# A two-layer decoder on one core: the first layer's film, modulation and spectrum go tile by tile into the selection loop, and its inverse, norms and feed forward are done per batch half

## The chip, the cores and the metric

The kernel runs on one core of a Trainium2 chip. The metric is the device time of one execution in microseconds, as the median of several runs. Engines: PE (matrix products), DVE (vector), ACT (scalar), POOL (GpSimd), SP (issues DMAs). Every engine has its own instruction stream, executes it in order, and waits on semaphores.

## The reference, cut to what matters

Two decoder layers over x (2 x 512 x 128) with a context of 2 x 154 x 96. The change lies in the second block of the first layer, and at its edges:

```python
scores = einsum('bthd,bghd->bhtg', Q, K) / sqrt(32)        # 4 heads, 154 keys
topv, topi = top_k(scores, 32); probs = softmax(topv)      # the selection
attn_mean = attn.mean(axis=1)
c_t = einsum('btg,bgd->btd', attn_mean, x_vision @ Wv) * text_mask
x = layernorm(x_text, g_norm_in, b_norm_in)
scale_in, shift_in = split(c_t @ W_film_in + b_film_in)    # film
x = x * (1 + mod_gate * scale_in) + mod_gate * shift_in    # modulation
y = irfft(rfft(x, 2L) * rfft(K, 2L))[:, :L] + x * D_skip   # K: taps from 64 states
y = y * (1 + mod_gate * scale_out) + mod_gate * shift_out
xt = x_text + y
h = gelu(layernorm(xt, g_ffn, b_ffn) @ W1 + b1) @ W2 + b2
return layernorm(xt + h, g_norm_out, b_norm_out)
```

After it come the outer norm, a mixture of experts over the same rows, and the second layer.

## The kernel before, in words

The 1024 rows are 8 tiles of 128 rows, tiles 0 to 3 being batch half 0 and tiles 4 to 7 half 1. PSUM is 8 banks of 512 columns. There is no scheduler: each engine's order is written out by hand in one function per stage, and the semaphores carry the dependences.

**Selection (b_pe_attention, b_dve_attention, b_act_attention).** Per tile, PE makes the scores (score, L658 and L660), ACT copies them (scores_in, L831), DVE finds each head's maximum (peak), ACT takes the exponentials (L841, L842), and DVE finds the 32 largest of each of 4 heads with rounds of max and match_replace (select), and makes probabilities (selected, shares; the last instruction of a tile is the reciprocal L808). ACT then makes four diagonal matrices (diagonals, L846 and L853), PE gathers the transposed attention (gather, L683 and L686), ACT copies it (attn_in, L902 and L903), PE multiplies by the film weights (film_tile, L708 and L709) and ACT copies the 512 film columns (film_in, L859). PE puts film_tile one tile behind, and a dummy product (stay_warm, L217) ahead of each gather.

**Taps.** Beside the selection ACT makes exponential and sine tables (low rates L497, high rates L504, waves L510 to L519), POOL multiplies them (L440 to L467), PE turns them into 512 taps (taps_of_lags, L669, at tile TAPS_AT = 5), ACT copies them in 16 small pieces (b_act_taps, L529), PE takes their spectrum (taps_spectrum, L721, with an outer product for D_skip, L723), and ACT weighs it (b_act_spectrum, L475).

**Modulation and spectrum.** POOL makes the affine norm u_n (L922 to L924) and modulates tiles 0 to 3 at once (L930, L931); DVE modulates tiles 4 to 7 (L987, L988) after the norm of the context (L982). PE takes the spectrum (L695) after all films.

**After it (b_pe_ssm, b_dve_ssm, b_act_ssm).** DVE multiplies the spectra in 4 groups of both halves (L996 to L1001), PE inverts (L939, L944, moving operand 256 columns), DVE applies the film (L1010 to L1013) and norms (stats L176, aggregate L179, variance L181, POOL's power L197, scaling L187), PE transposes (L209), ACT copies (L972), PE widens by W1 (L956), ACT takes gelu (L975), PE narrows by W2 (L963, the bias as an outer product L961), DVE adds and takes two norms per half (L1023 onward). PE meanwhile merges the experts' weights (c_pe, L1066 and L1072) and then transposes the rows (L209 again), which needs DVE's last norm: from there on the change touches nothing but a bank number.

Of the kernel before, what the change touches and what calls it, by code (L numbers as in the profile page):

```python
# [73 lines left out]
LINES = [("ffn_b2", 128), ("m_ob", 128), ("l_bo", 128), ("b_film", 512)]  # L74
# [23 lines left out]
def _build(nc, dram, ctx):  # L98
# [40 lines left out]
    ones_low = keep(64).bitcast(BF16)[0:1, :]  # L139
# [52 lines left out]

    def pool_rstd(pool, n=NT):
# [30 lines left out]
    def a_sp(sp):  # L224
# [9 lines left out]
        sp.dma_start(SB[0:1, r0 + 1024:r0 + 1024 + 896], dram["lines"]).then_inc(sem("small_in"), 16)  # L234
# [234 lines left out]
    def b_act_spectrum(act):  # L469

        act.wait_ge(sem("s_taps_dft"), 1)
        w = lambda j: ssm["bin_weight"][:, j:j + 1]
        for out, i in ((taps_re, 0), (taps_im2, 1), (taps_re2, 0)):
            for j in range(4):
                ins = act.activation(out[:, 128 * j:128 * j + 128], bank(i)[:, 128 * j:128 * j + 128], ACT.Copy, scale=w(j))  # L475
        ins.then_inc(sem("s_spectrum"), 1)
        act.wait_ge(sem("s_spectrum"), 1)
        act.activation(taps_re2[0:1, 0:128], bank(1)[0:1, 0:128], ACT.Copy, scale=w(0)[0:1, :])
        act.activation(taps_im2[0:1, 0:128], ones[0:1, :], ACT.Copy, scale=0.0).then_inc(sem("s_spectrum"), 1)

# [41 lines left out]
    def b_act_taps(act):  # L522
# [4 lines left out]
        for q in range(4):  # L527
# [74 lines left out]
    def b_pool_pre(pool, follow):  # L602
# [12 lines left out]
        follow(pool.tensor_copy(ones_low, ones[0:1, :]))  # L615
        follow(pool.tensor_scalar(skip_line, skip_line, 0.5, None, ALU.mult))
# [21 lines left out]
    hT = inner  # L638
    gelu = film


    FILMS = [[], [0], [1], [2], [3], [4], [5], [7]]
    TAPS_AT = 5

    def b_pe_attention(pe):
# [27 lines left out]
        def gather(t):  # L673

            if t >= 2:
                pe.wait_ge(sem("x_attn_in"), 2 * (t - 1))
# [3 lines left out]
            o = bank(4 + t % 2)  # L680
# [10 lines left out]
        def spectrum(part, j, b):  # L691

            mat = dft[("dft_cos", "dft_sin")[part]]
            for c in range(4):
                ins = pe.matmul(bank(4 * part + j)[:, 128 * b:128 * b + 128],  # L695
                                mat[:, 512 * c + 128 * j:512 * c + 128 * j + 128], uv[:, b, c], start=(c == 0), stop=(c == 3))
            return ins

        def film_tile(t):
# [5 lines left out]
            if t >= 2:  # L705
                pe.wait_ge(sem("x_film_in"), t - 1)
            b = t // (NT // B)
            pe.matmul(bank(6 + t % 2), attn0[:, 128 * t:128 * t + 128], vf0[:, 512 * b:512 * b + 512], start=True, stop=False)  # L708
            pe.matmul(bank(6 + t % 2), attn1[0:33, 128 * t:128 * t + 128], vf1[0:33, 512 * b:512 * b + 512], start=False,  # L709
                      stop=True).then_inc(sem("x_film"), 1)  # L710

        def taps_spectrum():

            pe.wait_ge(sem("x_scores_in"), NT)
            pe.wait_ge(sem("s_taps_copied"), 16)
            pe.wait_ge(sem("dft_in"), 16)
            for part, mat in ((0, dft["dft_cos"]), (1, dft["dft_sin"])):
                for j in range(4):
                    o = bank(part)[:, 128 * j:128 * j + 128]
                    for c in range(4):  # L720
                        ins = pe.matmul(o, mat[:, 512 * c + 128 * j:512 * c + 128 * j + 128],  # L721
                                        taps[:, 128 * c:128 * c + 128], start=(c == 0), stop=False)
                    ins = pe.matmul(o, mat[0:1, 128 * j:128 * j + 128], skip_line, start=False, stop=True)  # L723
# [1397 lines left out]
```

## Time and profile before

| what | value |
|---|---|
| median of 3 runs | 797.09 us (796.39 to 802.22) |
| profiled execution | 796.2 us |
| its span, first to last instruction | 794.1 us |
| mean granted clock of PE | 0.951 |
| PE busy | 713.8 us, 90% |
| DVE busy | 456.4 us, 57% |
| ACT busy | 279.5 us, 35% |
| POOL busy | 226.1 us, 28% |
| stretch that the change touches | about 36 to 220 us |

The span is the time between the first and the last instruction; what lies around it is 2.1 us. A view of a stretch starts its clock at the span's start. A float matrix product of 128 columns shows as two records, so that 8 records are 4 products. A start in one row and the start in the next give the time for which an engine is held; the duration in a row is a little longer where instructions overlap.

### The profile page before, as it was taken

What the parts mean: (1) busy time and instruction counts of PE and PEld (TensorE: products, weight loads), DVE (VectorE), ACT (ScalarE), POOL (GpSimd) and SP (SyncE); (2) the same over time, 40 slices, a digit from 0 to 9 for tenths busy, and PEclk for the clock granted to TensorE, in tenths of its full rate; (3) what the DMA queues carried; (4) which work ended last, traced back from release to release, by engine and by line L of the source; (5) the groups of instructions that cost most, each with busy time, mean ns of one, the idle gap of its engine ahead of it and who ended that gap; (6) DMA issues with size and microseconds to landing.
All of it is one profiled execution on the core that took longest, in us unless ns stands there. A gap on an engine that the chain in (4) does not pass through costs nothing.

```text
span 794.1 us, 8963 instructions
## 1 busy us (share of the span) xinstructions
PE 713.8 (90%) x3296; PEld 355.4 (45%) x3296; DVE 456.4 (57%) x1190; ACT 279.5 (35%) x527; POOL 226.1 (28%) x135
## 2 busy tenths in 40 slices
PE   8675879898989989999999999999977989999996
PEld 5232447774845433322222222227432354656555
DVE  7898890423626684576676767743664635333333
ACT  7998663003021004544444444430213204121220
POOL 4728710001201020435454554641635010000001
PEclk9867889999998999999999999999998989999999
DMA  8100050011000000000000000000500000000000
GB/s 314 32 0 1 1 213 1 1 60 47 1 1 0 1 0 0 1 1 0 1 1 0 1 1 0 1 1 1 225 1 0 1 1 1 1 0 1 1 0 28
DMA packets 3493, 18.67 MB, mean 24 GB/s; under 512 B 887, under 2 KB 2040, under 8 KB 2938
## 3 DMA queue, kind: packets, MB, share of 16 engines
q1 hardware_dynamic: 3450, 18.11, 5.9%
q8 instruction: 26, 0.43, 0.2%
q14 instruction: 17, 0.14, 0.1%
HBM read 17.58 MB, written 0.52 MB: 23 GB/s over the span
## 4 chain that ended last, share of the span: by engine, by line
PE 68%; DVE 14%; ACT 10%; issue 4%; POOL 3%; DMA 1%; POOLq 0%; DVEq 0%; SPq 0%; ACTq 0%
PE PS L1840 10%; PE PS L1323 7%; PE PS L1854 6%; DVE SB L1477 5%; PE PS L1307 4%; PE PS L1278 4%; PE PS L1291 3%; DVE SB L1226 2%; PE PS L695 2%; PE PS L217 2%; PE PS L1339 2%; PE PS L1361 2%; PE PS L1406 2%; PE PS L1638 2%; PE PS L1649 1%
## 5 line engine op out<-in xcount | busy, mean ns | idle before, releaser
L197 POOL TENSOR_TENSOR SB<-SB 128x4 f32<-128x4 f32 (+1 forms) x24 | 23.9, 997 | 371.6 <-DVE SB L181 371.5
L1460 POOL TENSOR_TENSOR SB<-SB 128x1024 f32<-128x1024 f32 x32 | 75.2, 2351 | 127.7 <-ACT SB L1430 127.6
L1477 DVE TENSOR_REDUCE SB<-PS 128x2 f32<-128x1024 f32 x64 | 78.5, 1226 | 52.7 <-PE PS L1291 52.6
L1430 ACT ACTIVATE SB<-PS 128x1024 f32<-128x1024 f32 x64 | 65.6, 1024 | 105.2 <-PE PS L1310 105.1
L217 PE MATMUL PS<-SB 128*128 128x512 f32 (+1 forms) x190 | 86.7, 602 | 1.5 <-DVE SB L294 1.1
L1840 PE MATMUL PS<-SB 128*128 128x512 f32 x176 | 82.5, 607 | 0.0
L1307 PE MATMUL PS<-SB 64*128 64x512 f32 x256 | 68.9, 616 | 0.0
L1323 PE MATMUL PS<-SB 128*64 128x512 f32 x256 | 67.8, 610 | 1.2 <-DVE SB L1514 1.2
L1510 DVE RECIPROCAL SB<-PS 128x512 f32<-128x512 f32 x16 | 53.7, 3358 | 17.6 <-PE PS L1339 17.6
L1920 DVE TENSOR_TENSOR SB<-SB,PS 128x512 f32<-128x512 f32 (+1 forms) x48 | 32.9, 688 | 52.7 <-PE PS L1840 48.9
L1878 ACT ACTIVATE SB<-PS 128x512 f32<-128x512 f32 (+1 forms) x48 | 28.5, 596 | 87.3 <-PE PS L1840 85.8
L1854 PEld LDWEIGHTS PS<-SB 128*128 128x128 f32 (+1 forms) x384 | 49.4, 190 | 18.5 <-issue 10.0
L1854 PE MATMUL PS<-SB 128*128 128x128 f32 (+1 forms) x384 | 54.5, 285 | 1.4 <-DVE SB L1920 1.4
L217 PEld LDWEIGHTS PS<-SB 128*128 128x128 f32 x190 | 36.2, 213 | 35.8 <-issue 32.5
L1840 PEld LDWEIGHTS PS<-SB 128*128 128x128 f32 x176 | 31.3, 189 | 33.4 <-issue 29.2
L1464 POOL TENSOR_TENSOR SB<-SB 128x1024 f32<-128x1024 f32 x16 | 37.6, 2348 | 1.3
L1278 PE MATMUL PS<-SB 128*128 128x512 f32 x64 | 35.8, 641 | 0.3 <-ACT SB L1413 0.3
L1307 PEld LDWEIGHTS PS<-SB 64*128 64x128 f32 x256 | 22.0, 187 | 27.2 <-issue 24.3
L1323 PEld LDWEIGHTS PS<-SB 128*64 128x64 f32 x256 | 14.4, 135 | 42.8 <-issue 33.0
L683 PE MATMUL PS<-SB 128*128 128x128 f32 x64 | 12.7, 362 | 18.6 <-ACT SB L853 18.6
L1291 PE MATMUL PS<-SB 64*128 64x512 bf16 x128 | 24.8, 384 | 4.6 <-DVE SB L1477 4.6
L1928 DVE SCALAR_TENSOR_TENSOR SB<-PS,SB 128x128 f32<-128x128 f32 x32 | 11.2, 351 | 30.3 <-PE PS L1854 30.3
(356 smaller groups left out, 1144.2 us busy)
## 6 DMA issues: line engine op xcount, KB each, us to landing
SB<-exp SPq DMA_DIRECT2D x1, 4352.0 KB, 13.2
SB<-moe SPq DMA_DIRECT2D x1, 4096.0 KB, 12.9
SB<-dft SPq DMA_DIRECT2D x1, 2304.0 KB, 11.6
SB<-att SPq DMA_DIRECT2D x1, 2048.0 KB, 8.1
SB<-mix SPq DMA_DIRECT2D x1, 768.5 KB, 4.7
SB<-mix SPq DMA_DIRECT2D x1, 640.0 KB, 5.8
SB<-ssm SPq DMA_DIRECT2D x1, 602.0 KB, 6.8
SB<-lat SPq DMA_DIRECT2D x1, 585.0 KB
```

The source lines that it names most:

```text
L217: pe.matmul(bank(b)[:, 0:moving.shape[1]], ones, moving, start=True, stop=True)
L1278: pe.matmul(bank(7), w[:, 128 * pair:128 * pair + 128], xsT[:, 512 * b:512 * b + 512], start=True, stop=True)\
L1291: ins = pe.matmul(bank(4 + h), qb_ring[i % 3][head(h), 128 * qt:128 * qt + 128], kb_ring[i % 3][head(h), :], start=True, stop=True)
L1307: pe.matmul(bank(2 * (n % 2) + h), k_ring[i % 3][head(h), 128 * u:128 * u + 128], q_ring[i % 3][head(h), :], start=True, stop=False)
L1323: ins = pe.matmul(bank(6)[head(h), :], v, expd[i % 2][:, 1024 * kt + 512 * h:1024 * kt + 512 * h + 512], start=(kt == 0), stop=(kt == 3))
L1430: act.activation(expd[i % 2][:, 1024 * u:1024 * u + 1024], bank(2 * (u % 2), 2), ACT.Exp).then_inc(sem("d_exp"), 1)
L1460: pool.tensor_tensor(half_sums[half], e[:, 0:1024], e[:, 1024:], ALU.add).then_inc(sem("d_half_sum"), 1)
L1464: pool.tensor_tensor(key_sum, half_sums[0], half_sums[1], ALU.add).then_inc(sem("d_key_sum"), 1)
L1477: dve.tensor_reduce(shift[i % 2][:, qt:qt + DK + 1:DK], two_heads(bank(4, 2)), AX_X, ALU.max, negate=True)\
L1510: dve.reciprocal(unit, bank(7)).then_inc(sem("d_unit"), 1)
L1840: pe.matmul(bank(2 * (i % 3) + side), exp_w["e_w13"][:, c:c + 128], xsT[:, 512 * n:512 * n + 512], start=True, stop=True).then_inc(sem(("t ...
L1854: ins = pe.matmul(bank(6 + j % 2)[:, 0:128], hidden[e % 2][0:m, T * k + 128 * t:T * k + 128 * t + 128], w2, start=(k == 0), stop=(k == FCH ...
```

## The change

The film of a tile follows its gather at once, all films in bank 6, all gathers in bank 4, and the dummy products in the selection are gone. POOL makes u_n ahead of its tap products and modulates tiles 0 to 6 one by one among them; DVE modulates tile 7 straight from PSUM. PE takes the spectrum tile by tile, accumulating over a half's tiles in two banks per half (5 and 7, 2 and 3), which a product with a row of zeros opens. The taps are made at tile 4 instead of 5, and ACT copies them in two groups of 8. D_skip is added to tap 0 by POOL. The taps' spectrum follows film 5 and DVE weighs it instead of ACT. Products, inverse, film, norm, transposes, widening, gelu and narrowing go per half; the inverse's moving operand is 128 columns. The stream x is added to the film's shift by POOL, POOL keeps the sum with the bias b2, and the outer products of D_skip and b2 are gone, for which the biases are now loaded to all 128 partitions. The second batch of low rates on ACT moves from tile 0 to tile 2. The context's norm on DVE comes after tile 7's modulation.

```diff
-        sp.dma_start(SB[0:1, r0 + 1024:r0 + 1024 + 896], dram["lines"]).then_inc(sem("small_in"), 16)
+        sp.dma_start(SB[:, r0 + 1024:r0 + 1024 + 384], dram["lines"][:, 0:384].to_broadcast([P, 384])).then_inc(sem("small_in"), 16)
...
+        follow(pool.memset(zeros_low, 0.0))
...
+    TAPS_AT = 4
+    SPECTRA = ((5, 7), (2, 3))
...
-            stay_warm(pe, 1, 4 + t % 2)
...
+        def spectrum(t):
+            b, c = divmod(t, 4)
+            if t < NT - 1:
+                pe.wait_ge(sem("s_u"), t + 1)
+            else:
+                pe.wait_ge(sem("s_u_late"), 1)
...
+            if c == 0:
+                for i in SPECTRA[b]:
+                    pe.matmul(bank(i), zeros_low, mask_low[:, 0:512], start=True, stop=False)
+            for part, mat in enumerate((dft["dft_cos"], dft["dft_sin"])):
+                for j in range(4):
+                    ins = pe.matmul(bank(SPECTRA[b][part])[:, 128 * j:128 * j + 128],
+                                    mat[:, 512 * c + 128 * j:512 * c + 128 * j + 128], uv[:, b, c], start=False, stop=(c == 3 and j == 3))
...
             if t == TAPS_AT:
                 taps_of_lags()
+                spectrum(1)
+                spectrum(2)
+            gather(t)
+            if t == 3:
+                spectrum(0)
             if t == NT - 1:
...
+                spectrum(4)
+            film_tile(t)
+            if t == TAPS_AT:
+                spectrum(3)
             if t == TAPS_AT + 1:
                 taps_spectrum()
...
+        for t in (5, 6, 7):
+            spectrum(t)
...
+            if t >= 2:
+                film_in(t - 2)
+            if t > TAPS_AT:
+                attn_in(act, t - 1)
...
             if t == TAPS_AT + 1:
-                b_act_taps(act)
+                b_act_taps(act, 2, 4)
             if t + 1 < NT:
                 exponentials(2 * t + 3)
-            if t >= 1:
+            if 1 <= t <= TAPS_AT:
                 attn_in(act, t - 1)
...
-            if t == 0:
+            if t == 2:
                 b_act_low_rates(act, 16, LOW)
             if t == 3:
                 b_act_high_rates(act)
+            if t == TAPS_AT:
+                b_act_taps(act, 0, 2)
         diagonals(NT - 1)
-        b_act_spectrum(act)
...
+        b_pool_high_factor(pool, follow, 0)
+        b_pool_high_factor(pool, follow, 1)
+        modulate(0)
+        b_pool_high_factor(pool, follow, 2)
+        b_pool_low_factor(pool, 0)
+        modulate(1)
+        b_pool_low_factor(pool, 1)
+        b_pool_high_factor(pool, follow, 3)
+        modulate(2)
+        modulate(3)
+        pool.wait_ge(sem("s_taps_copied"), 16)
+        pool.tensor_tensor(taps[0:1, 0:128], taps[0:1, 0:128], skip_line, ALU.add).then_inc(sem("s_taps_in"), 1)
+        modulate(4)
+        modulate(5)
+        modulate(6)
...
+        for b in range(B):
+            pe.wait_ge(sem("s_product"), b + 2)
+            if b == 1:
+                pe.wait_ge(sem("x_film_in"), NT)
+            y = bank(4 + 2 * b)
...
+        turn(0)
+        stay_warm(pe, 1, 0)
+        widen(0)
+        turn(1)
+        narrow(0)
+        widen(1)
+        narrow(1)
...
+        dve.wait_ge(sem("s_spectra"), 1)
+        products(0)
+
+        last = NT - 1
+        dve.wait_ge(sem("u_affine"), 1)
+        dve.wait_ge(sem("x_film"), NT)
+        follow(dve.tensor_tensor(tiled(u)[:, last], tiled(u_n)[:, last], bank(6)[:, 0:128], ALU.mult))
+        dve.tensor_tensor(tiled(u)[:, last], tiled(u)[:, last], bank(6)[:, 128:256], ALU.add).then_inc(sem("s_u_late"), 1)
...
+        dve.wait_ge(sem("s_spectra"), 2)
         dve.memset(dft["dft_sin"].rearrange("p (c l) -> p c l", c=4)[:, 1:4, 0:1], 0.0).then_inc(sem("s_product"), 1)
-
...
+        products(1)
...
+            follow(dve.tensor_tensor(tiled(inner)[:, tiles], four(bank(4 + 2 * b)), fv[:, tiles, 2], ALU.mult))
+            ins = dve.tensor_tensor(tiled(inner)[:, tiles], tiled(inner)[:, tiles], fv[:, tiles, 3], ALU.add)
+            ins.then_inc(sem("f_inner"), 1)
+            dve.wait_ge(sem("f_inner"), b + 1)
+            norm_half(dve, follow, tiled(inner), tiled(inner_n), b).then_inc(sem(("f_half", "f_normed")[b]), 1)
...
+            dve.wait_ge(sem("f_inner_kept"), k + 1)
             dve.wait_ge(sem("f_out"), k + 1)
...
+            follow(dve.tensor_tensor(xsum[:, c], xsum[:, c], bank(4 + 2 * k), ALU.add))
+            follow(norm_half(dve, follow, tiled(xsum), tiled(xn), k))
+            follow(dve.tensor_tensor(tiled(xn)[:, tiles], tiled(xn)[:, tiles], every(rows["g_out"]), ALU.mult))
+            follow(dve.tensor_tensor(xsum[:, c], xn[:, c], u_n[:, c], ALU.add))
+            norm_half(dve, follow, tiled(xsum), tiled(xs), k).then_inc(sem(("stage_half", "stage_done")[k]), 1)
...
-        sp.wait_ge(sem("s_conv"), 4)
+        sp.wait_ge(sem("s_conv"), 2)
```

norm_half is the norm of one half by the same instructions as before, with its own wait for POOL's power. POOL's list behind the selection (b_pool_ssm) is: x into the shift of half 0, the two powers of the context's norm, x into the shift of half 1, x plus b_out for all rows, then for each half the power and the sum with b2, then four powers.

## Rows read from the trace of the kernel before

**Rows 1.** Windows: us, busy of PE, PEld, DVE, ACT, POOL; clock, DMA, GB/s
```profile
36.00:53.00 17.00, 11.56 (x26) 5.22 (x27) 16.68 (x92) 16.16 (x60) 8.07 (x2) 0.50 0.00 0
...
205.60:220.00 14.40, 14.40 (x130) 12.76 (x130) 11.57 (x46) 1.02 (x1) 3.07 (x3) 1.00 0.01 1
```

**Rows 2.** Chain of work that ended last: start us, us, what
```profile
104.07 0.39 ACT SB L529
...
120.22 1.09 PE PS L721 x8
...
160.05 1.99 PE PS L939 x8
...
174.16 1.30 DVE SB L1010 x2
...
180.97 1.04 POOL SB L197
182.04 1.13 DVE SB L187 x4
...
185.16 7.15 PE PS L956 x16
...
205.60 7.15 PE PS L1066 x64
...
219.88 1.04 PE PS L209 x8
```

**Rows 3.** Timeline of DVE: start us, us, instruction, [idle before, releaser]
```profile
86.47 0.54 DVE L761 MAX8 SB<-SB 128x8 f32<-128x154 f32 x2 [1.95 <-ACT SB L831]
...
115.94 0.17 DVE L808 RECIPROCAL SB<-SB 128x4 f32<-128x4 f32 x1
...
199.70 0.69 DVE L1023 TENSOR_TENSOR SB<-SB,PS 128x512 f32<-128x512 f32 x1 [14.80 <-PE PS L963]
...
201.74 0.17 DVE L181 TENSOR_SCALAR SB<-SB 128x4 f32<-128x4 f32 x1
```

**Rows 4.** Timeline of ACT in the selection
```profile
57.43 1.90 ACT L510 ACTIVATE SB<-SB 128x2048 f32<-128x2048 f32 x1
...
79.26 0.60 ACT L859 ACTIVATE SB<-PS 128x512 f32<-128x512 f32 x1 [2.09 <-PE PS L709]
79.75 3.73 ACT L504 ACTIVATE SB<-SB 128x128 f32<-128x128 f32 x16
83.28 0.27 ACT L846 ACTIVATE SB<-SB 128x4 f32<-128x4 f32 x1
...
84.76 0.41 ACT L841 ACTIVATE SB<-SB 128x154 f32<-128x154 f32 x1
...
85.77 0.66 ACT L831 ACTIVATE SB<-PS 128x616 f32<-128x616 f32 x1
...
104.07 6.64 ACT L529 ACTIVATE SB<-PS 32x128 f32<-32x128 f32 x16 [1.89 <-PE PS L669]
```

**Rows 5.** Timeline of PE in the selection
```profile
85.00 2.05 PE L683 MATMUL PS<-SB 128*128 128x128 f32 x8 [2.83 <-ACT SB L853]
...
92.02 0.79 PE L658 MATMUL PS<-SB 128*128 128x308 f32 x2
...
94.88 1.05 PE L683 MATMUL PS<-SB 128*128 128x128 f32 x8
...
96.85 1.12 PE L708 MATMUL PS<-SB 128*128 128x512 f32 x2
...
98.96 2.14 PE L669 MATMUL PS<-SB 128*32 128x16 f32 x232
```

**Rows 6.** Timeline of POOL in the selection
```profile
62.63 7.44 POOL L453 TENSOR_TENSOR SB<-SB 128x2048 f32<-128x2048 f32 x2 [18.56 <-ACT SB L512]
...
83.72 4.54 POOL L458 TENSOR_TENSOR SB<-SB 128x2048 f32<-128x2048 f32 x1
...
99.81 1.10 POOL L930 TENSOR_TENSOR SB<-SB 128x512 f32<-128x512 f32 x1 [4.82 <-ACT SB L859]
```

More of the change, by code:

```diff
@@ L138, in _build @@
     key_bytes, key_columns = [bytes_in[r:r + 1, 2048:2048 + B * S2] for r in (0, DK)], bytes_in[:, NT:NT + 2 * B]
-    ones_low = keep(64).bitcast(BF16)[0:1, :]
+    ones_low, zeros_low = (keep(64).bitcast(BF16)[0:1, :] for _ in range(2))
     stream = Space(keep.at, keep.at + 4096)
@@ L526, in b_act_taps @@
         to = taps.rearrange("p (c g j) -> p c g j", c=4, j=4)
-        for q in range(4):
+        for q in range(a, z):
             for j in range(4):
@@ L858, in film_in @@
                 act.wait_ge(sem("s_low_products"), 3)
[L859 removed]
+            if t == NT - 1:
+                act.wait_ge(sem("s_u_late"), 1)
+            act.activation(film[:, 512 * t:512 * t + 512], bank(6), ACT.Copy).then_inc(sem("x_film_in"), 1)
         scores_in(0)
@@ L968, in b_act_ssm, with modulate @@
-    def b_act_ssm(act):
-        act.wait_ge(sem("turned"), 2)
-        act.wait_ge(sem("ffn_in"), 16)
-        act.wait_ge(sem("f_inner_kept"), 1)
-        act.activation(hT, bank(4, 2), ACT.Identity, scale=ffn["ffn_g"], bias=ffn["ffn_b"]).then_inc(sem("turned_in"), 1)
-        for k in range(4):
-            act.wait_ge(sem("f_hidden"), k + 1)
-            act.activation(gelu[:, T * k:T * k + T], bank(2 * (k % 2), 2), ACT.Gelu, bias=ffn["ffn_b1"][:, k:k + 1])\
-               .then_inc(sem("f_gelu"), 1)
+        def modulate(t):
+            pool.wait_ge(sem("x_film_in"), t + 1)
+            follow(pool.tensor_tensor(tiled(u)[:, t], tiled(u_n)[:, t], film[:, 512 * t:512 * t + 128], ALU.mult))
+            pool.tensor_tensor(tiled(u)[:, t], tiled(u)[:, t], film[:, 512 * t + 128:512 * t + 256], ALU.add).then_inc(sem("s_u"), 1)
@@ new lines, in b_act_ssm @@
+    def b_act_ssm(act):
+        act.wait_ge(sem("ffn_in"), 16)
+        for h in range(2):
+            c = slice(512 * h, 512 * h + 512)
+            act.wait_ge(sem(("x_half_turned", "turned")[h]), 2)
+            act.activation(hT[:, c], bank(5 + 2 * h), ACT.Identity, scale=ffn["ffn_g"], bias=ffn["ffn_b"])\
+               .then_inc(sem(("x_half_in", "turned_in")[h]), 1)
+            if h == 0:
+                act.wait_ge(sem("f_inner"), 2)
+            for k in range(4):
+                act.wait_ge(sem("f_hidden"), 4 * h + k + 1)
+                act.activation(gelu[:, T * k + 512 * h:T * k + 512 * h + 512], bank(k), ACT.Gelu, bias=ffn["ffn_b1"][:, k:k + 1])\
+                   .then_inc(sem("f_gelu"), 1)
@@ L1025, in b_dve_ssm @@
-        follow(norm(dve, follow, tiled(xsum), tiled(xn), prepare=add))
-        follow(dve.tensor_tensor(tiled(xn), tiled(xn), every(rows["g_out"]), ALU.mult))
-        follow(dve.tensor_tensor(xsum, xn, u_n, ALU.add))
-        norm(dve, follow, tiled(xsum), tiled(xs), first_half="stage_half").then_inc(sem("stage_done"), 1)
+            tiles = slice(4 * b, 4 * b + 4)
+            dve.wait_ge(sem("s_conv"), b + 1)
+            dve.wait_ge(sem("x_film_in"), 4 * b + 4)
+            dve.wait_ge(sem("s_shift"), b + 1)
@@ L1990, in _ @@
         b_pool_attention(pool, follow)
-        pool_rstd(pool, 4)
-        for _ in range(3):
-            pool_rstd(pool)
+        b_pool_ssm(pool)
         for _ in range(3):
```

247 lines of the change are left out of this document (119 added, 128 removed).

## Prediction

> **What bounds the kernel now.** I read the windows first, then the chain of work that ended last between 36 and 220 us, then the timelines of the four engines there. Up to tile 7 DVE's selection is nearly gapless: in the window 36 to 53 it is busy 16.68 of 17 us [rows 1], and its last reciprocal stands at 115.94 [rows 3]. But the chain leaves DVE at tile 5: the taps end on PE at 104.04, ACT begins 16 copies at 104.07 [rows 2], which last 6.64 us [rows 4], and tile 6's gather and the films queue behind them. From 120.22 PE works alone: the taps' spectrum, film 6, gather 7, the spectra. The inverse begins at 160.05, 44 us after the selection ended; it ends at 174.16, when DVE takes the film's product [rows 2]. Then DVE and PE take turns (film and norm, then the widening from 185.16). From 205.60 PE has 14.3 us of merging (two groups like that of 205.60, 7.15 us each) beside DVE's norms, and at 219.88 it transposes the finished rows [rows 2]. That start is the point where both kernels meet again: behind it the program is the same and TensorE sets the pace, so what it moves by, the end moves by.
>
> **Prices.** A product of 128x128 on 128 columns: 7.15 us for 64 records, so 0.2234 us each [rows 2]; where small products stand between, 1.09 us for 8 records, 0.2725 each at L721 [rows 2]. I take 0.2234 for runs of one kind (new inverse, narrowing, taps' spectrum, spectrum), since they are such runs, and keep 0.2725 for the range. With TensorE at full clock a gather is 1.97 us (94.88 to 96.85), a film 2.11 (96.85 to 98.96), a tile's scores 1.9 (from 92.02 to 94.88 stand they and a dummy of 0.96) [rows 5]; at half clock the first half of a gather is 2.05 instead of 1.0 at 85.00 [rows 5]. ACT: film copy 0.49, sixteen rates 3.53, diagonals 1.48, one pair of exponentials 1.0, scores copy 0.6 [rows 4]; attention copy about 0.35, an estimate from the width (film copy 0.49 is wider, twice 0.17 at least); a tap copy 0.415 [rows 4].
>
> **The start.** The bias load becomes a broadcast of 192 KB, and POOL gets one more memset. That delays POOL's list by 0.6 us or so by the volume; POOL, DVE and PE stand at most as late as ACT there, which is busy without a gap until it copies the first half of x. I take 0, at most 0.5.
>
> **Leg 1, to the end of the taps on PE.** ACT: 3.5 us of low rates leave tile 0; so the waves start when DVE's second tile lets them, about 1.4 us before 57.43 (1.9 gained, 0.5 for the film copy that now stands ahead). POOL: u_n (three instructions over 1024 columns, 6.6 us by twice the 1.10 for 512) goes into the 18.56 us of idle ahead of 62.63, which hides it; two modulations enter its products, 0.7 us each (from 1.10 us for 512 columns [rows 6]; 128 columns are between a quarter, 0.28, and 1.10 for each of two instructions, I take 0.35). POOL's products then end at 88.26 - 1.4 + 1.4 = 88.3 [rows 6]: unchanged, no bound. ACT in tile 3's turn: waves end at 67.9, exponentials and copy 1.35, low rates 3.53, diagonals 1.48, 2.1 for exponentials, scores and film, 1.35 again, high rates 3.53, diagonals 3 at 82.8. PE then does gather 3, spectrum 0, film 3, scores 7: 1.97 + 2.3 + 2.11 + 1.9 = 8.3 us warm, 16 us cold; PE stands idle for ACT ahead of gather 3, and the gather after such a wait ran at the lower clock at 85.00, so I add 2: the taps start at 93.1 and take 5.08 us as before (98.96 to 104.04, with the fetch in the middle [rows 2, 5]). They end at 98.2 instead of 104.04. Bounds 96.3 and 104.
>
> ACT waits for exactly that: its first 8 tap copies stand ahead of diagonals 4 and of the scores copy 7. DVE goes on with tile 5 (its exponentials are done) until about 96, then waits for the scores of tile 7 until about 104: some 7 us of DVE idle, against 1.95 and less now [rows 3]. The selection ends near 123 instead of 116. This is the price of the earlier taps, and PE's own queue hides it (next leg).
>
> **Leg 2, ACT to gather 5.** 8 x 0.415 = 3.3, diagonals 1.5, then the longer of gather 4 (2 to 4) and exponentials, scores copy, film copy (2.1), attention copy 0.35, taps 3.3, exponentials 1.0, diagonals 1.5: 13.1 + 0.7 = 13.8. Gather 5 starts at 112.0.
>
> **Leg 3, PE to the last spectrum.** Gather 5 3.0 (half cold), hand-over 0.45, film 5 2.1, taps' spectrum 32 x 0.2234 = 7.15 (12.0 before, 120.22 on, with the D_skip products), gather 6 1.97, hand-over 0.45, film 6 2.1, gather 7 2.0, opening products 0.5, spectrum 4 1.8, film 7 2.1, spectra 5 to 7 5.4: 29.0, end at 141.0. DVE's end of selection at 123 is 6 us ahead of gather 7 (129). Tile 7's modulation (0.5) is hidden by spectra 5 and 6; the taps' weights and half 0's products (2.3 + 4.1 on DVE: three and six instructions over 512 columns at 0.69 or less [rows 3], and small ones) stand beside gather 7 and film 7, the context's norm beside spectra 5 to 7. The inverse may start at 141.1, against 160.05: 19 us.
>
> **Leg 4, inverse.** 64 products x 0.2234 = 14.3 (14.1 before). Only 0.2 us dearer, with half 1's products (4.1) under half 0's inverse, and half 0's film and norm (below) under half 1's. Ends at 155.4.
>
> **Leg 5, to the transposes.** DVE per half: film 1.4, statistics to variance 1.4, power 1.04, scaling 1.13, 0.3 of hand-overs: 5.3 [rows 2, 3]. Before, the same for both halves stood between 174.16 and 183.2. Now PE does turn 0, a dummy and widening 0 (0.5 + 1.0 + 3.6 = 5.1; 7.15 for both halves [rows 2]) beside it; turn 1 ends at 5.9, narrowing 0 at 9.5, widening 1 at 13.1, its last gelu at 13.9 (0.6 for 512 columns, like the film copy), narrowing 1 at 17.4, merging at 31.7. Before it was 219.88 - 174.16 = 45.7: 14 us less. DVE has two chains of 0.7 + 3.8 + 1.35 + 3.8 = 9.7 from 9.5 on: 28.9, so 2.8 us before PE is done. POOL's list (powers 1.0, sums 1.15 each) fits between. The transposes start at 155.4 + 31.7 = 187.1.
>
> **The sum.** Some twenty hand-overs on the way that I priced at nothing, at 0.1 us: 2 us, so 189.3. That is 30.6 us before 219.88. The profiled execution took 796.2, giving 765.6; the median lies 0.9 above it, so 766.5, rounded to **767 us**.
>
> **The clock, row against rule.** The dummy products go away, and PE now waits for ACT between each gather and its film. In the window 36 to 53 TensorE has the lower level, 1.2 GHz (0.50), though the dummies are there; in 205.60 to 220 it has 2.4 GHz (1.00) after unbroken work [rows 1]. So the dummies don't hold the clock in the selection now, and losing them there costs little; from gather 5 on PE is unbroken. The Trainium skill, TensorE: Matmul & The Clock Gate (Part 1: The HAM clock gate), says that the throttled state is the default and that only activity releases it, and that a loop which waits between its groups of products starts each of them cold. The trace agrees at 85.00. By that rule alone every gather, film and spectrum of the selection would be cold; the rows' price for that is in the first rival.
>
> **Rivals.** *Cold selection.* Gather 3 to scores 7 cold is 6 us more than my 10.3 us, gather 4 and 5 add 2, a slow film or two 3: 11 us, 778. For it: 0.50 in rows 1, and less activity than before; against it: at 94.88 TensorE was warm inside the selection. *DVE or small prices decide behind it.* If the runs of 128 columns cost 0.2725, then the inverse, narrowing, taps' spectrum and spectra cost 3.1 + 1.6 + 1.6 + 1.5 = 8 more, and if POOL is late with a power, DVE's 2.8 us are used up: 774 to 778. *It doesn't do what it says:* the tap copies hold ACT so long that DVE, not PE, ends tile 7, and the films pile up at the end: the taps would have to end 6 us later than now, at 110, and only leg 5 is left with part of leg 3: 789 or so. *Slower:* from 83 to 187 about 80 us of PE's work are on the chain. If TensorE falls to 1.2 GHz and stays there, each such us costs another; from 31 us of them on the change loses, and with all of them it ends near 847. A trace with 1.00 from 205.60 to 220 under nearly the same work speaks against it [rows 1].
>
> **How the numbers follow.** Forecast 0.68 (760 to 774), cold selection 0.14, prices and DVE 0.11, not as told 0.04, slower 0.03. Low end: taps at 96.3, no hand-over cost, DVE in time: 767 - 2 - 2 and 3 for a warm gather 5 and shorter fetch, 760. High end: the two middle rivals at their prices and a little of both, 781. A measurement here tells about 1% from no change, so faster is below 789: 0.93; same 0.04; slower 0.03.
>
> **What the profile would show.** Right: the taps' products end near 98; an idle of about 7 us on DVE in front of a peak (L761's counterpart) near 96 to 104; the last spectrum ends near 141 to 143 and PE has no gap above 1 us from gather 5 to the merging except at the gelu; the last transposes start near 189, after the merging and not after DVE. Wrong: the granted clock under 0.8 between 105 and 160, DVE's last scaling later than PE's merging, or a start of the taps' products after 100.

## The result, and the profile after

| | kernel before | changed kernel |
|---|---|---|
| median | 798.08 us (796.39 to 802.22, 4 runs) | 773.31 us (773.11 to 774.70, 4 runs) |
| profiled execution, its span | 796.2, 794.1 us | 773.5, 771.7 us |
| mean granted clock of PE in it | 0.951 | 0.942 |
| transposes after the merging | 219.88 | 191.47 |
| from there to the end of the span | 574.2 | 580.2 |

The ratio is 0.9686, with an interval of 0.9645 to 0.9726. The forecast was 767, its range 760 to 781. Two single executions that ran in a slower state, one of the kernel before (820.55 us) and one of e5 (782.84 us), are left out of all times below. At the meeting point the change had won 28.4 us (30.6 forecast), 15.8 of them ahead of the inverse (it starts at 144.30 instead of 160.05) and 12.7 between there and the transposes; in the profiled executions 6.0 us of these were gone again at the end.

The windows first, over the stretches of [rows 1] and three more (columns: busy us and instructions of PE, weight loads, DVE, ACT, POOL; granted clock; DMA share; GB/s):

```profile
36.00:53.00 17.00, 12.34 (x31) 5.93 (x32) 16.72 (x91) 13.57 (x48) 14.82 (x5) 0.55 0.00 0
...
97.00:118.00 21.00, 14.14 (x165) 10.56 (x153) 12.15 (x68) 16.26 (x50) 2.09 (x5) 1.00 0.49 202
118.00:143.00 25.00, 24.49 (x173) 19.33 (x172) 18.79 (x70) 5.29 (x17) 7.13 (x9) 1.00 0.01 2
...
211.00:231.00 20.00, 19.20 (x59) 10.65 (x58) 11.54 (x40) 2.75 (x3) 2.04 (x2) 0.73 0.00 0
```

The selection has about the clock it had: 0.55, 0.72 and 0.80 in the windows 36 to 53, 53 to 72 and 72 to 97, against 0.50, 0.86 and 0.75 before. The critical stretch 97 to 143 runs at 2.4 GHz (0.85 and 0.99 before). But 211 to 231, behind the meeting point, stands at 0.73.

The timeline of PE answers to [rows 5] and to PE's part of [rows 2]:

```profile
95.32 2.20 PE L681 MATMUL PS<-SB 128*32 128x16 f32 x240
100.05 0.32 PE L681 MATMUL PS<-SB 128*32 128x16 f32 x16 [2.52 <-issue]
...
114.24 1.13 PE L694 MATMUL PS<-SB 128*128 128x128 f32 x8 [1.91 <-ACT SB L869]
...
137.41 5.62 PE L716 MATMUL PS<-SB 128*128 128x128 f32 x48
...
144.30 1.16 PE L998 MATMUL PS<-SB 128*128 128x128 f32 x8 [1.26 <-DVE SB L1090]
```

The taps' products start at 95.32 and end at 100.4, gather 5 starts at 114.24, the last spectrum ends at 137.41 + 5.62 = 143.0, and the inverse begins 1.26 us later. The timeline of DVE (the answer to [rows 3]) shows what was waited for:

```profile
107.14 0.54 DVE L777 MAX8 SB<-SB 128x8 f32<-128x154 f32 x2 [8.68 <-ACT SB L847]
...
140.63 3.58 DVE L187 TENSOR_SCALAR SB<-SB 128x96 f32<-128x96 f32 x2 [0.23 <-POOL SB L222]
...
162.97 1.88 DVE L208 TENSOR_SCALAR SB<-SB 128x128 f32<-128x128 f32 x4 [1.13 <-POOL SB L216]
```

DVE stands idle 8.68 us in front of a peak, as forecast (7). Two scalings are far too long: 3.58 us for a pair that took 0.57 just before, and 1.88 for four that took 1.13 in [rows 2]. The timeline of POOL (in [rows 6] its modulation stood at 99.81) says what ran beside them:

```profile
140.57 1.27 POOL L967 TENSOR_TENSOR SB<-SB 128x512 f32<-128x512 f32 x1
141.79 2.36 POOL L979 TENSOR_TENSOR SB<-SB 128x1024 f32<-128x1024 f32 x1
...
162.91 1.09 POOL L972 TENSOR_TENSOR SB<-SB 128x512 f32<-128x512 f32 x1
```

ACT, the answer to [rows 4]: in leg 1 it waits twice for PE, for the scores of tile 5 and for gather 2; in leg 2 it has two groups of copies of 3.31 us, where one of 16 copies took 6.64 before.

```profile
77.61 0.68 ACT L847 ACTIVATE SB<-PS 128x616 f32<-128x616 f32 x1 [1.57 <-PE PS L672]
...
81.37 0.28 ACT L922 ACTIVATE SB<-PS 128x128 f32<-128x128 f32 x1 [1.59 <-PE PS L697]
...
100.44 3.31 ACT L542 ACTIVATE SB<-PS 32x128 f32<-32x128 f32 x8 [10.26 <-PE PS L681]
104.11 1.28 ACT L869 ACTIVATE SB<-SB 128x128 f32<-128x128 f32 x4
...
108.14 3.31 ACT L542 ACTIVATE SB<-PS 32x128 f32<-32x128 f32 x8
```

The chain of waits from the inverse's end to the meeting point, for leg 5:

```profile
162.97 1.89 DVE SB L208 x4
...
165.56 3.57 PE PS L1025 x32
...
173.35 3.84 PE PS L1025 x32
177.19 7.15 PE PS L1152 x64
184.33 7.14 PE PS L1158 x64
191.47 1.04 PE PS L234 x8
```

Then the stretch in which the clock falls, in PE's timeline: sixteen products, by turns one row of ones by the bias `m_ob` (L1185) and the real product (L1186).

```profile
205.22 0.48 PE L1185 MATMUL PS<-SB 1*128 1x128 f32 x2 [1.06 <-DVE SB L1261]
205.63 0.49 PE L1186 MATMUL PS<-SB 128*128 128x128 f32 x2
...
207.72 0.48 PE L1185 MATMUL PS<-SB 1*128 1x128 f32 x2
208.13 0.80 PE L1186 MATMUL PS<-SB 128*128 128x128 f32 x2
...
213.91 0.80 PE L1186 MATMUL PS<-SB 128*128 128x128 f32 x2
214.50 6.39 PE L242 MATMUL PS<-SB 128*128 128x512 f32 x10
```

A row x2 is one product. Starts are 0.41 us apart up to 208.13 and 0.72 after it: the clock fell within the group, which took 9.28 us. The group is not the change's: in the kernel before it ran from 233.63 to 241.91, 8.28 us, and lost the clock after ten products instead of seven. A second group of the kind, the bias `l_bo` (L1758), loses it too, in both.

### The profile page after: what moved, and what is told of

It reads as the page before. It is cut to its first block, busy times and chain, and to the rows that moved or that the text cites. A ratio compares the mean times of both kernels' runs of the same rounds, so it can differ in the third digit from the quotient of the medians.

```text
span 771.7 us, 8984 instructions
## 1 busy us (share of the span) xinstructions
PE 695.4 (90%) x3300; PEld 345.8 (45%) x3300; DVE 459.3 (60%) x1183; ACT 277.0 (36%) x518; POOL 237.7 (31%) x154
## 4 chain that ended last, share of the span: by engine, by line
PE 69%; DVE 14%; ACT 9%; issue 4%; POOL 3%; POOLq 0%; DVEq 0%; ACTq 0%
PE PS L1926 11%; PE PS L1409 7%; PE PS L1940 6%; DVE SB L1563 5%; PE PS L1393 4%; PE PS L1364 4%; PE PS L242 3%; PE PS L1377 3%; DVE SB L1312 2%; PE PS L1425 2%; PE PS L1447 2%; PE PS L1492 2%; PE PS L1724 2%; PE PS L1735 1%; PE PS L670 1%
## 5 line engine op out<-in xcount | busy, mean ns | idle before, releaser
L222 POOL TENSOR_TENSOR SB<-SB 128x4 f32<-128x4 f32 (+1 forms) x18 | 17.8, 988 | 275.9 <-DVE SB L181 275.8
L242 PE MATMUL PS<-SB 128*128 128x512 f32 (+1 forms) x158 | 73.6, 619 | 1.5 <-DVE SB L319 1.1
L1926 PEld LDWEIGHTS PS<-SB 128*128 128x128 f32 x176 | 32.0, 193 | 34.1 <-issue 31.0
L242 PEld LDWEIGHTS PS<-SB 128*128 128x128 f32 x158 | 31.9, 224 | 32.1 <-issue 29.4
L1377 PEld LDWEIGHTS PS<-SB 64*128 64x128 bf16 x128 | 6.2, 93 | 47.6 <-DVE SB L1563 41.2
## 6 DMA issues: line engine op xcount, KB each, us to landing
SB<-moe SPq DMA_DIRECT2D x1, 4096.0 KB, 12.6
```

The lines of the kernel that those rows point to most:

```text
L242: pe.matmul(bank(b)[:, 0:moving.shape[1]], ones, moving, start=True, stop=True)
L1377: ins = pe.matmul(bank(4 + h), qb_ring[i % 3][head(h), 128 * qt:128 * qt + 128], kb_ring[i % 3][head(h), :], start=True, stop=True)
L1926: pe.matmul(bank(2 * (i % 3) + side), exp_w["e_w13"][:, c:c + 128], xsT[:, 512 * n:512 * n + 512], start=True, stop=True).then_inc(sem(("t ...
```

## The experiments

All start from the changed kernel, and "stretch" is the time from the transposes to the end of the span (580.2 in the profile of the changed kernel). A ratio is that to the kernel before, run beside it, with its 95% interval. Across the executions of the 12 kernels and of the kernel before, which ran beside them, one thing can be read: the time of one kernel follows its mean granted clock. The kernel before went from 796.15 us at 0.951 to 808.43 at 0.932; a line through its 27 executions falls about 6 us for each 0.01. So where it matters I also give a kernel's mean moved along that line to a clock of 0.945; there the kernel before is at 798.9 us. The line is rough (3 us between 0.951 and 0.942, 7 between 0.942 and 0.934), so a difference of 1 us between two such means says nothing.

### e8: the changed kernel again

> The changed kernel itself, run again beside the others. Theory (TensorE's clock falls at places that differ from execution to execution, and the length behind the meeting point goes with it): its times spread over some us, each time with its mean granted clock, the lower the longer, about 6 us for 0.01; the fastest reach 768. Rival (771.7 at 0.942 belongs to the kernel): all its times lie within 1 us of 773.5.

778.07 us (776.01 to 779.75), clock 0.934 to 0.942; ratio 0.9717 (0.9663 to 0.9770). At 0.945 the two sets of the changed kernel are at 771.5 and 772.2: the 4.8 us between their medians are clock. In this profile the taps' products ended at 104.76 instead of 100.4, with the same instructions: the window 53 to 72 is at 0.59 instead of 0.72, and ACT waited 3.71 us for PE's scores ahead of the waves instead of 0.33. All of it arrived at the inverse (148.71 instead of 144.30), and the transposes started at 195.81; the stretch was 580.6. So a start in one profile is good to about 4 us, and legs are compared, not starts. **At one clock the change is worth 27 us by the line.** Without the line it is 25.8 us at 0.942 (799.1 against 773.3) and about 28 at 0.934 (805.4 to 807.6 against 777.9 to 779.8).

### e1: POOL's sums held back from DVE's scalings

```diff
+        pool.wait_ge(sem("e_ctx_n"), 1)
         with_stream(1)
...
             pool.wait_ge(sem("f_inner"), k + 1)
+            pool.wait_ge(sem(("f_half", "f_normed")[k]), 1)
```

> The changed kernel, but POOL waits for DVE's scalings: the sum of x and the shift of half 1 and the sum with b_out come after the context's norm, and the two sums with b2 come after the scaling of their half. Theory (POOL's two-input instructions hold DVE's scalings off): the context's scaling of 3.58 us falls to about 0.6, the gap of 1.26 us ahead of the inverse to 0.2, the scaling of half 1 from 1.88 to 1.13; the transposes start near 189.5 instead of 191.5. Rival (the scalings were long for a reason of their own, such as waiting for their input): they stay long and the transposes stay at 191.5. The time follows by 2 us only if TensorE's clock behind the transposes stays as it is; it may move by some us either way.

774.57 us (768.36 to 778.87, clock 0.929 to 0.949), ratio 0.9670 (0.9566 to 0.9775); 770.6 at 0.945. The timeline of DVE and, below, of PE:

```profile
143.37 0.57 DVE L187 TENSOR_SCALAR SB<-SB 128x96 f32<-128x96 f32 x2
144.17 0.57 DVE L187 TENSOR_SCALAR SB<-SB 128x96 f32<-128x96 f32 x2 [0.23 <-POOL SB L222]
```

```profile
140.95 5.62 PE L716 MATMUL PS<-SB 128*128 128x128 f32 x48
146.76 1.16 PE L1000 MATMUL PS<-SB 128*128 128x128 f32 x8 [0.19 <-DVE SB L1092]
```

3.58 became 0.57 and the gap ahead of the inverse 0.19 instead of 1.26: the scaling is held while POOL's sums run, shown by moving the sums away. The second place won 0.77 us in PE's wait for the scaling of half 1, gave 0.41 back to a wait for the gelu and most of the rest elsewhere: from the inverse to the transposes it took 47.0 us against 47.2. About 1 us in all, and too little for the timing to confirm. The transposes themselves started at 193.77 and not at 189.5, because leg 1 was late in this profile: there the products of tile 2 and gather 3 ran at 1.2 GHz, with the window 72 to 97 at 0.59 instead of 0.80. PE's rows of e1 (the first half of gather 3 takes 2.08 us; in the changed kernel it stood at 86.95 and took 1.13, and the taps' products started at 95.32):

```profile
89.50 2.08 PE L694 MATMUL PS<-SB 128*128 128x128 f32 x8
...
99.30 2.21 PE L681 MATMUL PS<-SB 128*32 128x16 f32 x240
```

The Trainium skill, SBUF — State Buffer (Who interferes with whom), says that VectorE in a two-port mode, which a scaling can enter, and GpSimd exclude each other, the later one blocked for the whole instruction of the first. The trace agrees in that the scaling was held; both of POOL's instructions (3.6 us in a row) went first.

### e2: the taps at tile 5 again

```diff
-    TAPS_AT = 4
+    TAPS_AT = 5
```

> The changed kernel with the taps at tile 5 again. Theory: the earlier taps bring nothing of their own, since what ACT and DVE lose in waiting (10.3 and 8.7 us) they gain at the end: DVE's selection ends about 4 us earlier than 125.5, the taps' spectrum starts about 5 us later, and the last spectrum ends within 1.5 us of 143.0. Rival (the earlier taps are what shortens the stretch): the last spectrum ends 5 us later or more, as the taps do.

770.97 us (769.51 to 778.08, clock 0.934 to 0.948), ratio 0.9636 (0.9555 to 0.9718); 771.3 at 0.945, the changed kernel's 771.5. The taps' products ended at 104.5, 4.1 us later than in the changed kernel, and the inverse still began at 143.63, 0.7 sooner. The last spectrum ended within 1.5 us of 143.0, as the theory said. The earlier taps, my leg 1, are worth nothing by themselves.

### e3: the dummy products of the selection back

```diff
+            stay_warm(pe, 1, 4)
             pe.wait_ge(sem("x_probs"), ...)
```

> The changed kernel with one dummy product ahead of each gather again, as before. Theory (the dummies don't hold the clock in the selection): the long wait for ACT's waves still leaves film 1 and scores 5 at 1.2 GHz (2.1 us instead of 1.05 for the first film product), gather 5 and what follows get 1 us of dummy each where PE has no wait, and the inverse starts 1 to 3 us later. Rival (cold selection): the products from 70 to 81 us run at 2.4 GHz and the taps end 3 us or more earlier than 100.4.

776.51 us (776.21 to 777.67, clock 0.938 to 0.942), ratio 0.9691 (0.9622 to 0.9759); 773.7 at 0.945. The window 36 to 53 is at 0.58 instead of 0.55, and 72 to 97 at 0.82 instead of 0.80; the last spectrum ends at 145.79 instead of 143.03, with the taps' products where they were (100.55). In these two profiles the dummies bring no clock to the selection, and the last spectrum comes 2.8 us later with them. That doesn't settle the rival of the cold selection: without dummies the taps' products ended at 100.4 in one profile of the changed kernel and at 104.76 in the other (e8), and at 103.9 in e1, each time after more products at 1.2 GHz. With dummies there is one profile, so no run shows whether they would keep such executions away; the median with them, at one clock 1.5 to 2 us longer, gives no sign of it.

### e4: two more dummies ahead of the transposes

```diff
+        stay_warm(pe, 2, 7)
         turn_pe(pe, tiled(xs), 0, ...)
```

> The changed kernel with two more dummy products (2.1 us) between the merging and the transposes of the rows; nothing else changes. Theory (behind the meeting point TensorE's clock falls at other places when the same work starts at another time, and 6.0 us were lost so): the time from the transposes to the end is not 580.2 us again but another value between 574 and 583, so that the whole kernel is not slower by 2.1 us but by -4 to +5. Rival (the length behind the meeting point belongs to the changed kernel, by its memory or its DMAs): it is 580.2 within 0.5 us and the kernel is 2.1 us slower.

778.51 us (776.59 to 781.33, clock 0.932 to 0.941), ratio 0.9716 (0.9643 to 0.9788); 773.4 at 0.945, 1 to 2 more than the changed kernel. The merging ended at 195.85 and the transposes started at 197.60: TensorE, not DVE, sets that start, as the prediction had it. The stretch was 581.9 us and not 580.2, so the theory's "another value between 574 and 583" holds. That the 1.75 us put there arrive at the end agrees with the 1 to 2 us at one clock, but these are no more than the noise of such means.

### e5 and e6: a film's input ahead of the low waves, alone and with e1

```diff
                 b_act_high_waves(act)
+                attn_in(act, 1)
                 b_act_low_waves(act)
```

> The changed kernel, but ACT copies the attention of tile 1 between the high and the low waves instead of behind the wave stretch and tile 2's exponentials, so that PE's film 1 and scores 5 stand under the low waves. Theory (leg 1 is late because film 1 waits 12.4 us for that copy and then holds scores 5, gather 2 and DVE's maxima up at the lower clock): DVE's idle of 4.39 us near 74 to 78 falls to 3 or less, and the taps' products end 2 to 3.5 us earlier, near 97 to 98 where the clock is as in the changed kernel. Rival (ACT's own list sets leg 1, and PE's lateness is hidden): the taps end within 1 us of where they did. The time also moves with the clock granted behind, by up to 5 us either way.

> Both edits together: ACT's early copy for tile 1, and POOL standing aside for DVE's scalings. Theory: the two act in different legs and add: taps 2 to 3.5 us earlier, inverse 1.1 us nearer to the last spectrum, so the transposes near 187 to 188.5 against 191.4 at a like clock, median about 769. Rival (the clock is worth more than both): the median is not below that of the changed kernel run again beside it.

e5: 771.85 us (three executions, 770.53 to 781.63, clock 0.928 to 0.944), ratio 0.9676 (0.9585 to 0.9766); e6: 774.14 (770.91 to 776.94, clock 0.933 to 0.944), ratio 0.9656 (0.9591 to 0.9720). At 0.945 they are at 770.0 and 769.8, 1 to 2 below the changed kernel, about as much as its own two sets differ. Film 1 started at 68.20 instead of 70.03, but the taps' products ended at 102.3, not at 97 to 98. In e6 DVE's idle ahead of one tile fell from 4.39 to 2.36 us and grew from 8.68 to 12.83 ahead of the one behind the taps: what is won early on ACT is waited away there. Both profiles fell on executions of a low clock (the window 118 to 143 is at 0.80, and the inverse starts at 150.8 and 151.2), so their starts say little. By the means at one clock an earlier film input is worth 2 us at most; no profile shows it at a like clock.

### e7: the halves in line

```diff
-            dve.wait_ge(sem("s_conv"), b + 1)
+            dve.wait_ge(sem("s_conv"), 2)
```

> The changed kernel, but DVE starts the film product and norm of half 0 only when the inverse of both halves is done, so that this half's 5.3 us no longer stand under the inverse of half 1. Theory (the overlap of the halves is what leg 5 gains by): from the inverse's start to the transposes it takes 52 us instead of 47.1. Rival (leg 5 gains by the products left out, and the overlap is idle either way): within 1 us of 47.1.

785.09 us (two runs, clock 0.935), ratio 0.9806 (0.9726 to 0.9885); 779.0 at 0.945. From the inverse's start to the transposes it took 55.28 us instead of 47.17 (52 expected). So the overlap of half 0's film and norm with half 1's inverse is worth 8.1 us, 7 by the means at one clock, and is the largest piece of the change that one edit takes back. Part of the 8.1 is the clock: PE waited 6.14 us for half 0's scaling and then ran at 1.2 GHz, so that the first widening took 5.11 us instead of 3.70 and the window 165 to 192 is at 0.87 instead of 1.00.

### e9 and e10: the one-row products gone behind the meeting point

With the gain ahead of the meeting point explained, the six us behind it were open. e9 adds the bias on POOL and takes L1185 away; e10 is e9 with e1's waits.

```diff
-            pe.matmul(o, ones[0:1, :], lines["m_ob"][0:1, :], start=True, stop=False)
-            ins = pe.matmul(o, attended[:, 128 * t:128 * t + 128], mha["ow_T"], start=False, stop=True)
+            ins = pe.matmul(o, attended[:, 128 * t:128 * t + 128], mha["ow_T"], start=True, stop=True)
...
-            follow(dve.tensor_tensor(xsum[:, c], xs[:, c], bank(6 + k), ALU.add))
+            follow(dve.tensor_tensor(xsum[:, c], xsum[:, c], bank(6 + k), ALU.add))
...
+            pool.tensor_tensor(tiled(xsum)[:, half], tiled(xs)[:, half], lines["m_ob"][:, None, :].to_broadcast([P, 4, 128]), ALU.add)
```

> The changed kernel with the eight one-row outer products of m_ob ahead of the products by ow_T (L1185) gone from TensorE; POOL adds the bias to the stream right after the last scaling (two instructions over 512 columns, 1.15 us each, while DVE stands idle), and DVE adds the product to that sum. In the profile of the changed kernel the sixteen products stood from 205.22 to 214.50, 9.28 us, of them 0.41 us each at full clock for the first seven and 0.72 us each after it, and DVE's second add waited for the last. Theory (behind the meeting point TensorE sets the pace, and products with one row are what it does as the clock falls): eight products go, 3.3 us at full clock and up to 5.8 at half, so from the transposes at 191.47 to the end 585.2 - 3.3 to 5.8, that is 575 to 577 instead of 580.2, at a granted clock of 0.942; the median at clock 0.945 is 766 to 768. Rival (the loss behind the meeting point is not of these products, what they leave is filled by a clock that falls elsewhere): the stretch after the transposes stays at 579 to 581, and the median at clock 0.945 at 771.

> The same, with POOL's sums also held back from DVE's two-operand scalings as in e1_pool_aside. Both theories: 1.1 us between last spectrum and inverse less than in e9, and nothing from the scaling of half 1, so 0.5 to 1.5 us below e9 at the same granted clock: 765 to 767 at 0.945 by the first theory, 770 by the rival.

(The stretch meant in the first text is 580.2 less 3.3 to 5.8.) e9: 762.92 us (760.49 to 765.71, clock 0.948 to 0.957), ratio 0.9504 (0.9435 to 0.9573). e10: 761.92 (760.42 to 765.32, clock 0.946 to 0.955), ratio 0.9505 (0.9426 to 0.9584). The stretch is 567.6 and 567.7 us, 12.6 less, twice what the theory gave. At 0.945 the means are 767.5 and 766.5, inside what the first theory said for both and 4 to 5 below the changed kernel. PE's timeline in e9:

```profile
204.94 2.05 PE L1185 MATMUL PS<-SB 128*128 128x128 f32 x16 [1.06 <-DVE SB L1260]
206.83 4.46 PE L242 MATMUL PS<-SB 128*128 128x512 f32 x10
211.62 0.66 PE L234 MATMUL PS<-SB 128*128 128x128 f32 x4 [0.33 <-DVE SB L187]
```

Eight products take 1.89 us, 0.236 each, the five dummies 4.46 instead of 6.39, and the windows 211 to 231 and 231 to 251 are both at 1.00 (0.73 and 0.91 in the changed kernel; 0.91 and 1.00 in e10). Two effects, then: the time of the products, and the clock behind them.

### e11: full rows instead of one

```diff
-            pe.matmul(o, ones[0:1, :], lines["m_ob"][0:1, :], start=True, stop=False)
+            pe.matmul(o, ident, lines["m_ob"], start=True, stop=False)
...
-                pe.matmul(o, ones[0:1, :], lines["l_bo"][0:1, :], start=True, stop=False)
+                pe.matmul(o, ident, lines["l_bo"], start=True, stop=False)
```

> The changed kernel; the outer products of one row of ones by one bias row (L1185 and L1758) become products of the 128x128 identity by the bias on all 128 partitions: as many products, each as long, the same sum, but over 128 rows instead of one. What e9 took away was either eight products' time alone, or also what one-row products do to the clock. Theory (the clock falls because of the one-row products): the granted clock stays at 1.00 through both groups of sixteen products, all sixteen at 0.41 us each or 6.6 us a group, against 9.28 at L1185 in the changed kernel and 1.00 in e9 over the twenty us behind it; from the transposes to the end 574 to 577 instead of 580.2, median 767 to 770 at a mean clock of 0.95. Rival (the clock falls for want of work around them, in the waits and idle stretches of this stage, whatever the products hold): the second half of the sixteen is again at 0.72 us each, the stretch 580 as in the changed kernel, median 771 to 774 for a clock of 0.942.

761.20 us (756.95 to 761.92, clock 0.948 to 0.958), ratio 0.9495 (0.9425 to 0.9564); 764.6 at 0.945. PE's timeline:

```profile
209.86 0.49 PE L1185 MATMUL PS<-SB 128*128 128x128 f32 x2 [1.06 <-DVE SB L1261]
210.18 0.39 PE L1186 MATMUL PS<-SB 128*128 128x128 f32 x2
...
213.31 0.39 PE L1186 MATMUL PS<-SB 128*128 128x128 f32 x2
213.53 4.46 PE L242 MATMUL PS<-SB 128*128 128x512 f32 x10
...
604.34 0.39 PE L1759 MATMUL PS<-SB 128*128 128x128 f32 x2
```

Nothing is taken off TensorE, and the group of sixteen still takes 3.67 us instead of 9.28. Starts are 0.22 us apart instead of 0.41, at the same 2.4 GHz, so I was wrong that a one-row product costs as much as any other: by turns with a product over 128 rows, it makes both of them cost 0.41. It isn't the single row alone: where a product over 33 rows follows one over 128 (the two of a film, 512 columns, at 116.88 and 117.93 in the changed kernel) each takes 1.05 us, and 0.86 where all are over 128 rows (L1172 to L1174), again 0.19 more. And the granted clock stays: 211 to 231 at 1.00, 601 to 651 at 1.00 (0.73 and 0.83 in the changed kernel; 231 to 251 is at 0.91 in both). The stretch is 562.9 us, the shortest of all, 17.3 less than in the changed kernel. The Trainium skill, TensorEngine Tiling (Array Packing), Tiling Modes, Key Properties, says that going from one tiling mode to another drains TensorE. It doesn't say whether a product over one or 33 rows counts as another mode. If it does, a drain at each change would look as these rows do (0.19 us more each), but no run here separates a drain from another cost of the change.

### e12: e10, and the second group gone too

```diff
-                pe.matmul(o, ones[0:1, :], lines["l_bo"][0:1, :], start=True, stop=False)
...
+        pool.wait_ge(sem("stage_done"), 4)
+            pool.tensor_tensor(tiled(xsum)[:, half], tiled(xs)[:, half], lines["l_bo"]..., ALU.add)
         for k in range(5):
             pool.wait_ge(sem("e_norm2"), k + 1)
```

> e10_no_bias_aside, and the outer products of l_bo (L1758) are gone too: POOL adds that bias to the stream beside the attention of the second layer and DVE adds the product to it. They stood from 607.90 to 620.36 in the changed kernel, eight of 0.41 to 0.72 us. Theory: another 3.3 us at least, and the clock behind them no longer falls (window of 50 us behind them at 0.95 or more instead of 0.90 in e9), so 4 to 7 us below e10 (761.9): 755 to 758. Rival (these wait for DVE's product with the heads, so what they leave is waited away): 760 to 762.

760.43 us (757.52 to 762.66, clock 0.950 to 0.957), ratio 0.9496 (0.9436 to 0.9555): 1.5 below e10, not 4 to 7, with a stretch of 567.2 (567.7). From the group's start to the transposes behind it 11.1 us instead of 17.0 in e9, so the products' time was won. It was lost in front of them: POOL's two sums stand ahead of the powers of DVE's norms in its queue (L1665). The timelines of POOL and of PE in e12 (in e10 PE waited 1.52 us at this place, and the records behind it lasted 0.27):

```profile
536.79 2.50 POOL L1660 TENSOR_TENSOR SB<-SB 128x512 f32<-128x512 f32 x2
539.25 3.27 POOL L1665 TENSOR_TENSOR SB<-SB 128x8 f32<-128x8 f32 x2
```

```profile
550.43 0.47 PE L1689 MATMUL PS<-SB 128*128 128x128 f32 x1 [3.98 <-DVE SB L1816]
550.70 0.42 PE L1690 MATMUL PS<-SB 128*128 128x128 f32 x1
```

2.5 us of waiting, and then the products behind it at the lower clock. The clock behind the second group fell even so: its last four products took 1.35 us instead of 0.9, after a wait of 2.14 us. The median came out as the rival had it, but by another wait than the one that it named. At 0.945 it is at 765.6, no clear step from e10.

## Why the prediction was right, and where it was not

- **What bounds the kernel, and the meeting point.** Right: TensorE's merging ends at 191.47 and the transposes follow at once; e4 showed that TensorE, not DVE, sets their start. DVE was done 3 us earlier (2.8 forecast).
- **Leg 1.** The taps' products started at 95.32 instead of 93.1 and took 5.05 us (5.08 forecast), so they ended 2.2 late. The mis-sized term is ACT's list in tile 3's turn. It was added up with no wait for PE, but ACT waited 1.57 us for scores 5 and 1.59 for gather 2, which PE did at 1.2 GHz from 70.03 to 81; with waves that gained 0.7 us instead of 1.4, gather 3 started at 86.95, where 82.8 and the 2 us added for a cold gather make 84.8. The gap of 2.5 us inside the taps' products is in both kernels; the prediction calls it a fetch, for which no run shows the reason. The earlier place itself was worth nothing (e2), which the prediction had not asked.
- **Legs 2 to 4.** 13.8 us (13.8), 28.8 (29.0), 14.6 (14.3). The price of 0.2234 us for runs of one kind held, so the rival of small prices falls. The taps' spectrum took 7.25 us instead of 12.0 without its one-row products. The price of 0.2725 in [rows 2] is theirs: four products behind a one-row product take three times 0.2234 and once 0.41 or so, which makes the 1.09 read there (e11).
- **Between leg 3 and the inverse.** 0.1 forecast, 1.27 measured: "the context's norm beside spectra 5 to 7" was costed at nothing, and POOL's sums held its scaling (e1).
- **Leg 5.** 32.6 instead of 31.7, which is 13.1 us less than before (14 forecast). The second scaling was held by POOL for 0.76, but e1 shows that little of this reaches the transposes. The overlap of halves, which hides half 0's film and norm, is worth 8.1 us (e7).
- **The allowance of 2 us for hand-overs** met 2.2 + 1.2 + 0.3 + 0.9 - 0.2 = 4.4 us of misses. With a slip in the sum (187.1 and 2 are 189.1, not 189.3) the meeting point was 2.2 us late. Of the signs named in advance, "no gap above 1 us" failed at the inverse (1.26), and in e4 and e8 the taps' products started after 100, which was to be a sign of being wrong.
- **What is shown and what is read.** e7 takes back the overlap of the halves, and e2 and e3 show that the place of the taps and the missing dummies carry little (0 and about 2 us). No run takes back film and spectrum tile by tile, to which most of the 15.8 us ahead of the inverse belong; that part is read from the two traces alone.
- **The step that failed:** "behind it the program is the same ... so what it moves by, the end moves by". The program is the same and the time isn't: 574.2 us before, 580.2 after. All of it is TensorE at 1.2 GHz in three places: 1.5 us at the group of sixteen and its five dummies, 1.4 at the four dummies that come next, and 3.1 around the second group. The runs speak against a cost of the change: the same stretch took from 575.5 us (e1) to 582.0 (e7) in kernels that are equal there, and the profile of before, 796.2 us at 0.951, is as fast as the fastest of 27 other executions, whose median is 799.1. But there is only this one profile of the kernel before, so what its stretch takes at a lower clock isn't shown. Against the 799.1 the 8 executions of the changed kernel, median 775.4, are 24 us faster, and at one clock 26 to 28. What the prediction lacked is the scatter: it carried the time of one execution at a favourable clock over to the median of another kernel, where 0.01 of clock is about 6 us. That the first set fell 6 us from the forecast and the second 11 is in part luck of the clock; both lie in the range.
- **The clock, row against rule.** The row was right for the profiles that ended the taps near 100.4; in others (e1, e4, e6, e8) more of the selection ran at 1.2 GHz, the taps ended 3.4 to 4.4 us later and the inverse moved with them, so the cold selection comes in some executions. A slower end through TensorE at 1.2 GHz happened in small, 6 us instead of 80, and not where the rival put it but where neither the change nor the prediction looked.

## What to carry to other kernels

A bias as a product of one row of ones is not cheap on TensorE: by turns with real products each cost 0.41 us instead of 0.22, and the clock fell within every group of sixteen that alternates so. The same sum as a product by the identity (e11), or on an idle engine ahead of time (e9), took 12 to 17 us off the stretch behind the meeting point and 10 to 12 off the median, 4 to 7 of it at one clock and the rest through the clock. Before a profile's own time is carried to a median, look at the clock of the other runs. And what is moved onto POOL belongs behind what others wait for in its queue, and not beside DVE's scalings.

## What the runs showed of the hardware

- One kernel's executions spread over 12 us, and their granted clock with them (796.15 at 0.951, 808.43 at 0.932). The profiles show three places where equal instructions meet a different clock: the selection (72 to 97 at 0.80 in the changed kernel, 0.59 in e1), the stretch 118 to 143 (1.00, but 0.80 in e5 and e6 and 0.84 in e11, where the inverse starts at 148.9 to 151.2 instead of 144.30, in part by this), and the groups of sixteen, where it fell after 10, 7, 9, 10, 6, 7, 4, 3, 6 and 4 products in the profiles of before, the changed kernel, e8, e1, e2, e3, e4, e5, e6 and e7.
- Products over 1 and over 128 rows by turns: 0.415 us each at 2.4 GHz and 0.72 at 1.2; all over 128 rows: 0.2234 at 2.4. Why the clock falls in the first kind stays open. With full rows it held in both groups (e11). But in the kernel before, the taps' spectrum and the narrowing had one such product to four and kept 1.00 (120 to 132, 193.5 to 205.4), and in e12 the clock fell in the second group though its one-row products were gone.
- DVE's scaling beside POOL's two-input sums: 3.58 us instead of 0.57, and 1.88 instead of 1.12.
- The taps' products (16 columns, 256 records) have one gap of 2.0 to 2.6 us in them in every profile, in which PE waits for nothing shown.
